# Another start and other orders for a kernel of attention, adapters and a recurrence

## What is computed

```python
y   = x @ W[subject].T + b[subject]                    # per item one of 8 weights of 256x256
q, k, v = y @ Wq.T + bq, y @ Wk.T + bk, y @ Wv.T + bv  # 16 heads of 16
sim = q k^T / 4 / (|temperature| + 0.1)                # within an item
s   = sum over 5 freqs of alpha * sin(2 pi sim / freq + phi)
w   = sigmoid(s);  w = w / (sum(w) + 1e-10)
x1  = x + layernorm((w v) @ Wo.T + bo) * gamma + beta
h   = relu(x1 @ W1[lang] + b1[lang]) @ W2[lang] + b2[lang]
z   = layernorm(x1 + h) * gamma[lang] + beta[lang]
for each of the 32 items in turn, state c over 64 tokens:
    f, i, g = sigmoid(z wf + c uf + bf), sigmoid(z wi + c ui + bi), tanh(z wc + c uc + bc)
    c = f * c + i * g
out = x1 + tanh(z wo + c_final @ uo + bo)
```

## Time and profile before

| | us |
|---|---|
| median of three runs | 389.83 |
| lowest and highest | 389.05, 392.76 |
| the profiled execution's own time | 389.83 |
| its span, first to last instruction | 388.1 |
| PE busy | 309.9 (80%) |
| DVE busy | 298.2 (77%) |
| ACT busy | 288.7 (74%) |
| POOL busy | 27.9 (7%) |
| chain that ended last: ACT, PE, DVE, SP's queue | 28%, 26%, 16%, 14% |

### The profile page before, as it was taken

One profiled execution on the slowest core, in us unless ns is written; L12 is line 12 of the kernel. 1 busy time (PEld: TensorE's weight loads), 2 busy tenths in 40 slices (PEclk: granted clock), 3 DMA queues, 4 the chain that ended last, 5 costly groups with the idle time before them and its releaser, 6 DMA issues.

```text
span 388.1 us, 6640 instructions
## 1 busy us (share of the span) xinstructions
PE 309.9 (80%) x2276; PEld 174.6 (45%) x2276; DVE 298.2 (77%) x641; ACT 288.7 (74%) x422; POOL 27.9 (7%) x42
## 2 busy tenths in 40 slices
PE   4656686586488779899697797989978898888885
PEld 3435333444236445553354554546554444443333
DVE  3007678994979999889866899999999999756244
ACT  0228699978699999989959598998999988232222
POOL 6000000000010002040000001110100010001000
PEclk9986789968799999899989699999999999999999
DMA  5334646465172330005303230022031021000006
GB/s 148 114 78 107 184 109 179 113 169 202 31 209 54 74 73 1 2 0 139 55 2 52 77 90 2 2 70 52 11 84 35 2 62 49 1 2 0 0 2 216
DMA packets 31717, 27.65 MB, mean 71 GB/s; under 512 B 12227, under 2 KB 25667, under 8 KB 31684
## 3 DMA queue, kind: packets, MB, share of 16 engines
q1 hardware_dynamic: 31684, 27.23, 25.9%
HBM read 23.02 MB, written 2.10 MB: 65 GB/s over the span
## 4 chain that ended last, share of the span: by engine, by line
ACT 28%; PE 26%; DVE 16%; SPq 14%; issue 9%; DMA 5%; POOL 1%; POOLq 0%; DVEq 0%; ACTq 0%
ACT ang L912 7%; SPq L282 6%; ACT ang L903 6%; PE pg L559 5%; DVE sc L1383 4%; PE pf L406 4%; PE pf L475 2%; ACT L909 2%; ACT sc L918 2%; PE pg L552 2%; SPq L262 2%; PE pr L571 2%; DMA uout<-in_uout 2%; ACT L916 2%; DMA wc<-in_cond 2%
## 5 line engine op out<-in xcount | busy, mean ns | idle before, releaser
L1383 DVE SCALAR_TENSOR_TENSOR sc<-ang,small,sc 128x512 f32<-128x512 f32 (+1 forms) x160 | 98.6, 639 | 1.3
L912 ACT ACTIVATE ang<-ang,qs 128x2560 f32<-128x2560 int32 x32 | 77.5, 2426 | 2.9 <-DVE ang L1368 2.8
L903 ACT ACTIVATE ang<-sc,phase 128x512 int32<-128x512 f32 (+1 forms) x140 | 78.4, 625 | 1.0 <-DVE sc L1383 0.9
L559 PE MATMUL pg<-gate_u,cT 128*64 128x384 f32 x256 | 50.0, 513 | 6.7 <-DVE cT L1490 6.4
L552 PE MATMUL pg<-gate_w,zT 128*64 128x384 f32 x256 | 47.3, 492 | 2.8 <-ACT pg L940 1.6
L1368 DVE TENSOR_SCALAR ang<-ang 128x2560 int32<-128x2560 int32 x32 | 47.4, 1486 | 2.0 <-ACT ang L903 1.9
L475 PE MATMUL pf<-qm,kT 128*64 128x256 f32 x256 | 33.9, 409 | 13.6 <-issue 9.2
L944 ACT ACTIVATE gat<-pg 128x384 f32<-128x384 f32 x32 | 15.5, 483 | 30.4 <-PE pg L559 30.4
L1359 DVE TENSOR_SCALAR ang<-sc,phase 128x512 int32<-128x512 f32 (+1 forms) x60 | 24.0, 427 | 14.2 <-ACT sc L894 14.1
L475 PEld LDWEIGHTS pf<-qm,kT 128*64 128x64 f32 x256 | 18.5, 142 | 25.4 <-issue 16.7
L559 PEld LDWEIGHTS pg<-gate_u,cT 128*64 128x64 f32 x256 | 16.9, 141 | 27.5 <-issue 17.0
(11 more groups left out here) (113 smaller groups left out, 461.2 us busy)
## 6 DMA issues: line engine op xcount, KB each, us to landing
wc<-in_cond SPq DMA_DIRECT2D x32, 257.0 KB, 2.9
wa<-in_down SPq DMA_DIRECT2D x32, 66.0 KB, 1.8
w<-in_up SPq DMA_DIRECT2D x32, 64.2 KB, 2.1
xt<-in_xt SPq DMA_DIRECT2D x8, 256.0 KB, 3.2
b<-in_up_b SPq DMA_DIRECT2D x32, 64.0 KB, 2.1
out_t<-go SPq DMA_DIRECT2D x8, 256.0 KB, 2.3
xg<-in_x SPq DMA_DIRECT2D x3, 512.0 KB, 5.2
qm<-qT SPq DMA_DIRECT2D x48, 32.0 KB, 2.1
```

The costliest lines, as they stand in the source:

```text
L559: mm = pe.matmul(pg[n % 2][u * L:(u + 1) * L, 0:GCOLS], cT[:, kc, :], gate_u[:, kc, u, :], start=False, stop=(kc == KC - 1), skip_group_ch ...
L903: op = act.activation(ang[:, n % SLOTS, f, r], unit(n)[:, r], ACT.Identity, scale=TURN / FREQS[f], bias=phase[:, p * NF + f:p * NF + f + 1])
L912: act.activation(a.bitcast(F32), a, ACT.Sin, scale=2 * PI_LOW / TURN, bias=qs[:, 3:4]).then_inc(sine_ready, 1)
L1383: op = dve.scalar_tensor_tensor(out=unit(n)[:, r], in0=sine, scalar=amp, in1=unit(n)[:, r], op0=ALU.mult, op1=ALU.add)
```

## The change

- The queries of group 0, half c=0, are no longer spread by DMA. DVE multiplies five heads' copies by a mask with one column for each head, and ACT three (`mask_queries` on each; the mask is a sum over blocks of the unit matrix). All other spreads stay DMAs.
- ACT issues the weight loads of items 2 and 3 of group 0 on its own queue, and loads its first table right after. The unit matrix is loaded ahead of the small constants.
- PE multiplies the unit matrix with itself, into a tile that nobody reads at that time: eight times ahead of the first conditioning, and three times each ahead of the first turn, the first queries and the first scores.
- `ON_ACT` falls by seven angles in all, four in group 0 and three in group 4; these are DVE's now.
- Conditioning, values, output projection, input gates, output part and kept output become two calls each, and `residual`, `moments` and `modulated` on DVE are cut in two at the point where DVE waited for its own result.
- The lists of all four engines are written anew. On SP the eight constants of the later stages move from behind group 1's second spread to ahead of its first; `load_rest(0)` goes behind that spread; the loads of quarter 6 stand ahead of those of quarter 5. In ACT's list the scaling of those constants (`halved`) moves forward, and 20 table loads stand in `sines` and `weights`. In DVE's list `centre_output_weights` moves ahead of the first angle, and `shifted(5)` stands behind step 17 and not behind step 16.

The diff, without the greater part of the lists:

```diff
-ON_ACT = [3, 4, 3, 4, 3, 4, 3, 4, 3, 4, 3, 4, 3, 4, 3, 4, 3, 4, 3, 4, 3, 4, 3, 4, 3, 4, 3, 4, 3, 4, 3, 4]
+ON_ACT = [2, 2, 3, 3, 3, 4, 3, 4, 3, 4, 3, 4, 3, 4, 3, 4, 3, 4, 3, 4, 3, 4, 3, 4, 3, 4, 3, 4, 3, 3, 3, 2]
...
+MASKED_BY_DVE = 5
...
             sp.dma_start(ids[:, :], ids_in).then_inc(ids_s, 16)
-            sp.dma_start(small[:], small_in).then_inc(small_s, 16)
             sp.dma_start(eye[:], eye_in).then_inc(eye_s, 16)
             load_x(0)
+            sp.dma_start(small[:], small_in).then_inc(small_s, 16)
             sp.wait_ge(ids_s, 16)
-            for j in range(SIZES[0] // 2):
-                load_cond(0, j)
+            load_cond(0, 0)
             sp.dma_start(wq[:], wq_in).then_inc(qk_s, 16)
             sp.dma_start(wk[:], wk_in).then_inc(qk_s, 16)
             load_attention_consts()
-            sp.wait_ge(setup_pool, 1)
-
-            spread_q(0, 0)
+
+            load_cond(1, 1)
             load_cond(1, 0)
             load_x(1)
             spread_q(0, 1)
-            load_cond(1, 1)
+            load_cond(1, 2)
             load_cond(1, 3)
-            load_cond(1, 2)
+            load_rest_consts()
+            spread_q(1, 0)
+            load_cond(2, 0)
             load_rest(0)
-            load_cond(2, 0)
-            spread_q(1, 0)
-            load_cond(2, 3)
             load_cond(2, 2)
             load_x(2)
+            spread_q(1, 1)
+            load_cond(2, 3)
+            load_cond(2, 1)
             load_rest(1)
-            load_cond(2, 1)
-            spread_q(1, 1)
-            load_rest_consts()
             load_cond(3, 1)
+            load_cond(3, 3)
             load_cond(3, 2)
+            spread_q(2, 0)
+            spread_q(2, 1)
+            load_x(3)
+            load_rest(2)
             load_cond(3, 0)
-            load_x(3)
-            spread_q(2, 0)
-            load_rest(2)
-            spread_q(2, 1)
-            load_cond(3, 3)
+            load_x(4)
+            load_cond(4, 0)
             load_cond(4, 1)
+            spread_q(3, 0)
             load_rest(3)
-            spread_q(3, 0)
+            load_rest(4)
             spread_q(3, 1)
-            load_rest(4)
-            load_cond(4, 0)
-            load_x(4)
-            load_rest(5)
             spread_q(4, 0)
             spread_q(4, 1)
             load_rest(6)
+            load_rest(5)
             load_rest(7)
...
-            def condition(q):
+            def condition(q, h):
 
                 g = GROUP[q * PB]
-                if q * PB == FIRST[g]:
+                j = 2 * q - FIRST[g] // 2 + h
+                if j == 0:
                     pe.wait_ge(x_loaded, g * 16 + 16)
                     wait(pe, s_copied, FIRST[g])
-                for j in (2 * q - FIRST[g] // 2, 2 * q - FIRST[g] // 2 + 1):
-                    pe.wait_ge(wc_loaded[j], 32 * sum(SIZES[k] > 2 * j for k in range(g + 1)))
-                    for kc in range(KC):
-                        for row, b in halves(j):
-                            mm = pe.matmul(pft[row:row + L, j, :], xg[:, kc, b * L:(b + 1) * L], wc[:, b, kc * D:(kc + 1) * D],
-                                           start=(kc == 0), stop=(kc == KC - 1))
+                pe.wait_ge(wc_loaded[j], 32 * sum(SIZES[k] > 2 * j for k in range(g + 1)))
+                for kc in range(KC):
+                    for row, b in halves(j):
+                        mm = pe.matmul(pft[row:row + L, j, :], xg[:, kc, b * L:(b + 1) * L], wc[:, b, kc * D:(kc + 1) * D],
+                                       start=(kc == 0), stop=(kc == KC - 1))
                 mm.then_inc(cond_done, 1)
...
                 if t % tc == 0:
-                    pe.wait_ge(qm_loaded, (g * KC + c + 1) * 16 * HC)
+                    if n == 0:
+                        pe.wait_ge(qm_dve, 1)
+                        pe.wait_ge(qm_act, 1)
+                    wait(pe, qm_loaded, (g * KC + c) * 16 * HC)
...
-            condition(0)
+            for _ in range(8):
+                pe.matmul(pct[:, :], eye[:, :], eye[:, :], start=True, stop=True)
+            condition(0, 0)
+            condition(0, 1)
+            for _ in range(3):
+                pe.matmul(pct[:, :], eye[:, :], eye[:, :], start=True, stop=True)
             turn_tokens(0)
+            for _ in range(3):
+                pe.matmul(pct[:, :], eye[:, :], eye[:, :], start=True, stop=True)
             queries(0, 0)
             queries(0, 1)
             keys(0, 0)
             keys(0, 1)
+            for _ in range(3):
+                pe.matmul(pct[:, :], eye[:, :], eye[:, :], start=True, stop=True)
             scores(0)
...
                 if c == 0:
-                    wait(act, qm_loaded, g * KC * 16 * HC)
+                    wait(act, qm_loaded, (g * KC - 1) * 16 * HC)
...
+            def mask_queries():
+                act.wait_ge(q_ready, 1)
+                act.wait_ge(setup_pool, 1)
+                act.wait_ge(mask_ready, 1)
+                nb = SIZES[0]
+                for h in range(MASKED_BY_DVE, HC):
+                    op = act.activation(qm[:, 0:nb, h % 2, h // 2, :], qT[:, 0, 0:nb * L].rearrange("p (b n) -> p b n", n=L),
+                                        ACT.Identity, scale=mask[:, h:h + 1])
+                op.then_inc(qm_act, 1)
...
+            act.wait_ge(ids_s, 16)
+            for j in range(1, SIZES[0] // 2):
+                for b in (2 * j, 2 * j + 1):
+                    s = act.value_load(ids[0:1, b:b + 1], min_val=0, max_val=NSUB - 1)
+                    act.dma_start(wc[:, b, :], cond_in[bass.ds(s, 1)].rearrange("a p n -> p (a n)")).then_inc(wc_loaded[j], 16)
+            act.preload_act_table_set("silu_and_others")
             act.wait_ge(small_s, 16)
             act.wait_ge(setup_dve, 1)
 
             tokens(0)
             queries(0, 0)
             queries(0, 1)
+            mask_queries()
             keys(0, 0)
             keys(0, 1)
             copy_scores(0)
             copy_scores(1)
-            angle(0, 2)
             angle(0, 3)
             angle(0, 4)
-            angle(1, 1)
             sines(0, True)
+            angle(1, 3)
+            angle(1, 4)
             copy_scores(2)
             copy_scores(3)
...
+            dve.wait_ge(eye_s, 16)
+            dve.tensor_reduce(mask[:, :], eye[:, :].rearrange("p (h r) -> p h r", r=HD), mybir.AxisListType.X, ALU.add).then_inc(mask_ready, 1)
...
+            def mask_queries():
+                dve.wait_ge(q_ready, 1)
+                dve.wait_ge(setup_pool, 1)
+                dve.wait_ge(mask_ready, 1)
+                nb = SIZES[0]
+                for h in range(MASKED_BY_DVE):
+                    op = dve.tensor_scalar(qm[:, 0:nb, h % 2, h // 2, :], qT[:, 0, 0:nb * L].rearrange("p (b n) -> p b n", n=L),
+                                           mask[:, h:h + 1], None, ALU.mult)
+                op.then_inc(qm_dve, 1)
...
                 for j in range(2):
                     op = dve.scalar_tensor_tensor(out=x1[:, 2 * q + j, :], in0=tiles(q)[:, j, :], scalar=rs[:, q % 2, j:j + 1], in1=rows[:, 0, :],
                                                   op0=ALU.mult, op1=ALU.mult)
-                link(op)
+                op.then_inc(x1_part, 1)
+
+            def residual_added(q):
+                dve.wait_ge(x1_part, q + 1)
                 dve.wait_ge(xt_ready, q + 1)
                 dve.tensor_tensor(x1[:, part(q)], x1[:, part(q)], xt[:, q % 2], ALU.add).then_inc(x1_ready, 1)
...
-            def moments(q):
+            def adapted(q):
                 dve.wait_ge(base_ready, q + 1)
                 dve.wait_ge(up_done, q + 1)
-                link(dve.tensor_tensor(b2[:, q % 2], tiles(q), b2[:, q % 2], ALU.add))
+                dve.tensor_tensor(b2[:, q % 2], tiles(q), b2[:, q % 2], ALU.add).then_inc(x2_ready, 1)
+
+            def moments(q):
+                dve.wait_ge(x2_ready, q + 1)
...
-                link(dve.tensor_tensor(z, chunks(q).rearrange("p c (b n) -> p c b n", n=L), of_language(q, 0), ALU.mult))
+                dve.tensor_tensor(z, chunks(q).rearrange("p c (b n) -> p c b n", n=L), of_language(q, 0), ALU.mult).then_inc(z_part, 1)
+
+            def shifted_language(q):
+
+                dve.wait_ge(z_part, q + 1)
+                z = zT[:, q % 2].rearrange("p c (b n) -> p c b n", n=L)
                 dve.tensor_tensor(z, z, of_language(q, 1), ALU.add).then_inc(z_ready, 1)
...
             conditioned(0)
+            mask_queries()
+            centre_output_weights()
             angle(0, 0)
             angle(0, 1)
+            angle(0, 2)
             wrap(0)
             values(0)
             angle(1, 0)
-            centre_output_weights()
+            angle(1, 1)
+            angle(1, 2)
             add_sine(0, 0)
             add_sine(0, 1)
             add_sine(0, 2)
+            wrap(1)
             angle(2, 0)
             add_sine(0, 3)
             add_sine(0, 4)
             angle(2, 1)
             angle(3, 0)
-            wrap(1)
-            conditioned(1)
```

(42 more changed lines are left out.)

1081 lines of the change are left out of this document (570 added, 511 removed).

## The result

| us | before | after |
|---|---|---|
| median of the runs | 390.25 (four, 389.05 to 392.76) | 365.36 (four, 363.12 to 366.25) |
| the profiled execution, its span | 389.83, 388.1 | 366.25, 364.5 |
| ratio, 95% interval | | 0.9346 [0.9282, 0.9409] |
| first angle on DVE | 29.34 | 20.79 |
| from there to the end of the last quotient | 308.0 | 292.0 |

The last three lines split the spans: 8.5 us come from the start and 16.0 from the middle, and the tail gives 1.0 back. Medians and ranges in this document are over all executions, while the ratios leave out those that were counted as slow, so the two can differ by up to 1%.

What follows compares the result with a forecast made beforehand. It took DVE and ACT, both 88% busy, to bound the middle, with chains ahead and behind. From 388.1 us, -7.8 start, -5.5 middle and -0.5 tail gave 374.3 of span, 376.0 of time; range 367 to 386.

Steps and rivals of the forecast that it cites:

- The start: Chain up to DVE's first angle: that angle at 21.5 us instead of 29.34, -7.8 us, bounds -3.5 and -8.6.
- comes up somewhere in the conditioning: PE's clock in the start: rises during the conditioning, not before it, which put the first angle at 21.5 us.
- rival (d): Start: unit matmuls don't lift PE's clock, slow through first scores; first angle 25.8, 4.3 later, time 380.3 us; chance 0.10.
- Rival (a): Middle: PE's order or the recurrence sets the pace, half the start is lost; 385.8 us; chance 0.20, including towards it.
- The middle: DVE's ledger behind the first angle: 4.2 angles, -2.4 centring, -1.4 pairs, -5.9 idle time, sum -5.5 us.
- I take half, -5.9: DVE's idle in the middle: half of 11.7 us waiting for uout, yT and xt goes, bounds 0 and -14.
- Splitting ... adds no instruction: Finer pieces of conditioning, values, projections and gates: gain inside the half of idle time already taken, no own term.
- the pairs' -1.4: DVE, three dependent pairs in each of eight quarters pulled apart: 0.06 us each, -1.4 us, bounds 0 and -2.9.
- Group 1: SP's weight loads for group 1: last lands at about 34 us, ten earlier, removing idle time without moving the end by ten.
- The tail: Behind 337.4 us: same work on PE, only the last transpose stands behind less, -0.5 us, bounds -2 and +1.
- Rival (b): Whole kernel: start at its bound, idle waits gone whole with 14 us, and links; 365.6 us; chance 0.15, including towards it.
- Rival (c): SP issues quarter 6's loads ahead of quarter 5's: DVE waits for xt, 0 to 2 us expected, worst 395.1; chance 0.05.

Runs made afterwards that it cites:

- experiment 1: Kernel before the change with only the new start, the old orders, coarse pieces and share of angles kept: 382.42 us, ratio 0.9749.
- experiment 8: Changed kernel with all split halves on PE and DVE's pairs put back together, run twice: 375.00 us (0.9538) and 373.58 us (0.9582).
- Experiment 2: Changed kernel without its 17 unit matmuls: 369.25 us, ratio 0.9416.
- experiment 4: Changed kernel with all four first weight loads of group 0 on SP's queue: 363.41 us, ratio 0.9204.
- experiment 3: Changed kernel with group 0's first half spread by eight DMAs again: 370.20 us, ratio 0.9393.
- experiment 9: Changed kernel with some halves rejoined: DVE's pairs 365.49 us, PE's halves 368.60, PE's input gates with DVE's pairs 369.37.
- experiment 7: Changed kernel with the seven angles moved back from DVE to ACT: 365.30 us, ratio 0.9319.
- experiment 12: Changed kernel with quarter 5's loads ahead of quarter 6's on SP: 360.82 us, ratio 0.9205.
- experiment 13, best version: Changed kernel with group 1's second spread ahead of quarter 0's loads and quarter 5's loads ahead of quarter 6's on SP: 359.08 us, ratio 0.9168.
- 10: Changed kernel with group 1's second spread ahead of quarter 0's loads on SP, DVE taking quarter 0's x later: 362.01 us, ratio 0.9222.
- experiment 5: Kernel before the change with the new start and SP's whole new list, other engines' lists old: 383.29 us, ratio 0.9799.
- experiment 6: Changed kernel with the eight constants loaded behind group 1's second spread again: 387.37 us, ratio 0.9858.

## Why the prediction was wrong in size and right in kind

It said faster, by 13.8 us; it was 24.9. Experiments 1, 8 and the changed kernel cut the 24.9 in three: by their ratios the new start is 10 us (7 to 12), the new orders with coarse pieces 6.5 to 8.5, the finer pieces 7.5 to 9.5.

**The start: right.** -7.8 was forecast and the first angle came 8.5 earlier, at 20.79, the bound that I had worked out for PE fast (20.7). Of its terms, the unit matmuls' cost was put at 0.4 and was nothing: their sixteen instructions took 2.74 us, not 3.9, and ended at 8.66, ahead of the landing. The landing itself I had put at 8.8, and it was 9.22: it was issued at 5.12, as worked out, and took 4.10 us, not 3.6. That the two errors cancelled was luck. So was much of the landing: in the other profiles with two queues it lies between 8.65 and 10.04. That the clock "comes up somewhere in the conditioning" was too careful by 0.7 us in all. Experiment 2 comes near rival (d): first angle 25.62 for the 25.8 worked out, and 3.9 us in the time, where (d) had 4.3. But (d) had the keys fast and the scores slow, and it was the other way round, so the match is in part luck. The second queue's gain, a term of this sum through the landing, was 0.3 us by experiment 4, because with one queue half of the conditioning is done ahead of the last landing. The masks are worth 5.9 us at the first angle (experiment 3) and the units 4.8 (experiment 2), more together than the 8.5 of the whole start, for without either PE is slow in part of the chain; the early table load, 1.28 us in the chain before, wasn't tried alone.

**The head start passes: right.** Rival (a) falls by experiment 1: the new start by itself brings as much as its first angle comes earlier.

**The middle: the failed step.** -5.5 was forecast and -16.0 came. The step that failed is the one that reads "I take half, -5.9" of the idle time named. The idle time fell by 12.8 us, and two things were missing. First, I let only the waits count that showed in three rows; the view of waits had 6.3 us more for the adapters, which went too. By that view 17.6 us of these 18.0 are gone, and 4.1 more of the 5.7 that DVE waited for sines from ACT. Against them stand 4.8 more for ACT's angles, 1.6 for scores and 2.8 for the weighted values: a net of 12.5 of the 12.8. The next waits showed, as I had said, and took 9.2 of 21.7 us, but the sum over all kinds, not a half of three, is what counts.

Second, "Splitting ... adds no instruction ... its gain is inside the half just taken" gave the pieces no term. By experiment 8 they are worth 8.5 us: about a third of it is less busy time on DVE, which I had as the pairs' -1.4 with -2.9 as the bound (2.3 by experiment 9, 3.4 by experiment 8), the rest shorter waits in the middle and a shorter tail.

The other terms of the ledger: seven angles to DVE were +4.2, which is 3.0 in DVE's busy time and nothing in the time (experiment 7), 0.42 each where I had 0.61; both engines had idle time to take them, DVE 25 us and ACT 34. The centring of the output weights did move ahead of the first scores, at 16.68 to 19.1. DVE's busy time came out at 267.2 for the 271 expected.

**Group 1.** As forecast: its conditioning runs at 31.88 to 35.56, and no yT waits.

**The tail.** -0.5 was forecast, +1.0 measured, within the bounds; it holds quarter 6's scaling and z and one step of the recurrence, which stood ahead of the last quotient before.

**Rival (b)** gave 365.6 and the time was 365.36. Its start was right. Its middle was right in sum only: it had the waits named gone with 14 us, and what happened was 21.7 us of waits gone, half of which I had not named, and 9.2 new. That the totals meet within 0.3 us is luck.

**Rival (c)** was real. I expected 0 to 2 us of it, and experiment 12 puts it at 4.5 (3 by experiment 13 beside 10), of which the rows show 0.45 and 1.35 on DVE, behind 2.12 on PE: I had followed xt alone, and the adapters' weights stand behind it in the same queue.

**Not settled.** How much of the orders' 6.5 to 8.5 us belongs to which list: SP's alone brings nothing (experiment 5), and the others lose more than 20 when only the constants go back (experiment 6), so they can't be taken apart. What of the pieces works only together with DVE's pairs stays open too.

PE's clock had no term in the forecast for the middle, and no experiment holds it fixed. Behind the first angle PE is busy for 293.5 us before (2212 instructions) and 289.0 after (2218), and the granted clock of the middle is 0.93 before and 0.95 after (0.96 in the second profile). Over whole executions the changed kernel has 0.955 to 0.976, and with the halves together 0.945 to 0.966. Executions of one kernel differ with it too: with the halves together 368.82 us came with 0.966, and the four of 373.11 to 377.05 with 0.945. How much of the gain of orders and pieces is this clock, and whether shorter waits raise it or the clock shortens the waits, isn't shown.

## What to carry to other kernels

In a kernel of in-order engines where none is full, sum the idle time by kind of wait, short ones too, before you price a reordering: the three long waits that caught the eye were 11.7 of 37.6 us here, and 21.7 went. Cutting work on PE and dependent pairs on DVE into pieces, with no instruction more, was worth 8.5 here, so it needs a term of its own. A queue's order and the orders of the engines that wait for it may pay only together, as here; of a moved load, follow everything that is queued behind it to its reader. If the first chain runs on PE behind idle time, unread work ahead of it can pay: here eight matmuls cost nothing, as they ended 0.56 us ahead of the load waited for, and the conditioning behind them ran at nearly twice the rate. Before you bring a landing forward, ask what can be done ahead of it.

## What the runs showed of the hardware

The granted clock reads 1.00 in the first 20.8 us of the changed kernel, and it does so too over the start of experiment 2, while sixteen instructions of the conditioning take 1.95 us in the one and 3.68 in the other. In these stretches only the durations show which of the two levels (1.2 and 2.4 GHz) PE has. The setup's twelve took 0.244 each, the units behind them 0.171 on average: the clock rose while they ran. "TensorE: Matmul & The Clock Gate" of the Trainium skill, section "What's actually happening", has the half speed as the default that sustained activity lifts. Experiment 2 agrees, with 3.68 against 1.95 us, and so does the fall to 3.25 behind 3.98 us of idling in experiment 3.

A second queue brought the last landing forward by less than the issue: issued 2.2 us earlier, it took 4.10 us instead of 3.18 with one queue (experiment 4) and was in 1.2 us earlier. In the chains of the other profiles with two queues it took 3.54 to 4.94 us. The time has nothing of it: 365.36 us with two against 363.41 with one, 359.08 against 360.19 on the best version. "DMA: Bandwidth & Descriptors" of the Trainium skill, section "Issuing engines are not separate DMA queues", has both feed the same 16 engines, with the sequencer's time as all there is to save. The trace agrees: no more than the 2.2 us came forward, and 0.9 of them went into the longer landing.

The executions of one kernel lie 1 to 8 us apart, and the changed kernel's two profiled ones had middles of 292.0 and 288.5 us with the same work. Two dependent DVE instructions back to back cost more than the same two with another between: the same 568 instructions keep DVE busy for 269.4 to 270.6 us with the pairs together and for 267.2 to 268.1 with the pairs apart (0.1 us a pair). Differences of 2 us between two versions are not told apart here.
